# Rows laid out by position modulo four in a macaron block of routed experts and dilated attention

## The reference

```python
x = x + 0.5 * ffn(layernorm(x))      # "job" m = 0..7 in the kernel
x = x + long_attention(layernorm(x)) # "long"
x = x + 0.5 * ffn(layernorm(x))      # "job" m = 8..15

def ffn(x):                          # per sequence
    q, k, v = split(x @ w_qkv)       # 16 heads of 8
    o = softmax(causal(q k^T / sqrt(8))) v
    h = layernorm(x + o @ w_o) * g1 + b1
    w = top 2 of 8 experts of softmax(h @ wg), rescaled to sum 1
    moe = sum over the two: w * (gelu(h @ w1 + bb1) @ w2 + bb2)
    return layernorm(h + moe) * g2 + b2

def long_attention(x):               # q = k = v = x, one head of 128
    # the 256 positions split by position modulo 4 into 4 sets of 64;
    # each set: softmax(xs xs^T / sqrt(128)) xs, divided by 4
```

## Time and profile before

| | |
|---|---|
| median of 3 runs | 1218.78 us (1218.28 to 1222.53) |
| profiled execution | 1228.96 us, its span 1227.1 us |
| mean granted TensorE clock | 0.893 |
| TensorE matmuls | 1042.0 us busy, 85% of the span |
| TensorE weight loads | 837.6 us, 68% |
| VectorE | 693.5 us, 57% |
| ScalarE | 655.5 us, 53% |
| GpSimd | 586.3 us, 48% |
| DMA | 181.01 MB, mean 148 GB/s |

### The profile page before, as it was taken

The page is one execution under the profiler, slowest core; times in us unless marked ns, Lnnn a source line. Parts: engine busy times, 40 slices in busy tenths (PEclk is TensorE's granted clock), DMA queues, the critical chain, the costliest instruction groups (busy, mean ns, idle before and its releaser), DMA issues.

```text
span 1227.1 us, 29800 instructions
## 1 busy us (share of the span) xinstructions
PE 1042.0 (85%) x10977; PEld 837.6 (68%) x10977; DVE 693.5 (57%) x2452; ACT 655.5 (53%) x1478; POOL 586.3 (48%) x711
## 2 busy tenths in 40 slices
PE   4888979998989989898989979898899988776660
PEld 3566647886867777686767867787777866676660
DVE  6548656563568745685558835786557723520413
ACT  1233425774666656675656746666566747343240
POOL 2224455236555545546464555656364466443415
PEclk9878979997989988898988989999889979888685
DMA  4492116655545646544555545545456546576561
GB/s 80 97 210 60 37 35 171 196 164 147 155 151 133 187 117 171 137 124 162 147 145 156 159 127 148 161 147 172 127 158 174 169 138 180 165 247 221 169 213 45
DMA packets 116471, 181.01 MB, mean 148 GB/s; under 512 B 12360, under 2 KB 79464, under 8 KB 116328
## 3 DMA queue, kind: packets, MB, share of 16 engines
q1 hardware_dynamic: 108136, 162.32, 46.9%
q0 software_dynamic: 8192, 16.79, 4.8%
HBM read 145.10 MB, written 38.68 MB: 150 GB/s over the span
## 4 chain that ended last, share of the span: by engine, by line
PE 72%; DVE 8%; another core or an unknown queue 6%; issue 6%; ACT 5%; POOL 2%; DMA 1%; POOLq 0%; ACTq 0%; DVEq 0%
PE ps_ring L569 15%; PE ps_ring L578 12%; PE ps_quad L440 8%; PE ps_quad L473 6%; PE ps_quad L469 6%; PE ps_ring L486 5%; PE ps_quad L446 3%; PE ps_ring L490 2%; ACT probs L653 2%; PE ps_ring L413 2%; PE ps_ring L501 2%; PE ps_ring L560 2%; PE ps_ring L420 1%; POOL picked L1107 1%
## 5 line engine op out<-in xcount | busy, mean ns | idle before, releaser
L1045 POOL TENSOR_SCALAR_AFFINE_SELECT probs<-probs 128x512 f32<-128x512 f32 x256 | 178.7, 707 | 272.2 <-ACT probs L653 265.9
L653 ACT ACTIVATE probs<-ps_quad 128x768 f32<-128x768 f32 x256 | 194.0, 806 | 162.5 <-PE ps_quad L473 100.6
L689 ACT ACTIVATE act<-ps_ring,weights 128x128 f32<-128x128 f32 x736 | 201.8, 385 | 123.9 <-PE ps_ring L569 90.1
L816 DVE TENSOR_REDUCE shift_cols<-ps_quad 128x2 f32<-128x512 f32 (+3 forms) x256 | 149.9, 586 | 153.5 <-PE ps_quad L454 117.8
L578 PE MATMUL ps_ring<-weights,act 128*128 128x128 f32 x1472 | 202.3, 286 | 35.1 <-ACT act L689 18.8
L569 PE MATMUL ps_ring<-tile_t,weights 128*128 128x128 f32 x1472 | 199.6, 293 | 17.0 <-ACT tile_t L680 8.8
L578 PEld LDWEIGHTS ps_ring<-weights,act 128*128 128x128 f32 x1472 | 185.1, 199 | 38.5 <-ACT act L689 20.6
L569 PEld LDWEIGHTS ps_ring<-tile_t,weights 128*128 128x128 f32 x1472 | 185.7, 205 | 31.1 <-issue 18.3
L1107 POOL DMA_INDIRECT picked<-sorted_outputs,place x128 | 123.2, 962 | 81.9 <-issue 81.6
L941 DVE TENSOR_TENSOR tile_y<-ps_ring,weights 128x128 f32<-128x128 f32 x184 | 51.1, 287 | 191.8 <-PE ps_ring L578 97.5
L1094 POOL DMA_INDIRECT sorted_rows<-h_rows,place x128 | 124.0, 969 | 52.3 <-issue 34.5
(11 more groups left out here) (132 smaller groups left out, 1532.2 us busy)
## 6 DMA issues: line engine op xcount, KB each, us to landing
weights<-expert_weights SPq DMA_DIRECT2D x184, 578.0 KB
tile_rows<-sorted_rows SPq DMA_DIRECT2D x56, 192.0 KB
sorted_outputs<-tile_y SPq DMA_DIRECT2D x56, 192.0 KB
query_key_parts<-qk SPq DMA_DIRECT2D x32, 256.0 KB, 4.8
k<-query_key_parts SPq DMA_DIRECT2D x64, 64.0 KB
q<-query_key_parts SPq DMA_DIRECT2D x64, 64.0 KB
sorted_rows<-zeros SPq DMA_DIRECT2D x2, 1472.0 KB, 10.7
xs<-in_L_attn_x SPq DMA_DIRECT2D x8, 256.0 KB, 5.6
```

The lines of the kernel that those rows point to most:

```text
L653: sc.activation(probs[:, r % PROBS, 2 * a:2 * a + 2, :], ps_quad[:, 2 * a:2 * a + 2, 0:3 * P], ACT.Exp, scale=HD ** -0.5).then_inc(pair_fr ...
L689: ins = sc.activation(act[:, k % ACTS, f, :], bank(use)[:, f * P:(f + 1) * P], ACT.Gelu_apprx_tanh, bias=weights[:, k % WEIGHTS, 2 * F + f ...
L816: dve.tensor_reduce(shift_cols[:, late, groups], ps_quad[:, groups, 0:split], AX.X, ALU.max)
L1045: pool.affine_select(out=both, in_=both, compare_op=ALU.is_ge, fill=0.0, base=0, pattern=[[0, 2], [0, 2], [1, P]], channel_multiplier=-1). ...
```

## The change

Partition 64g + n of row tile 2q + h now holds position 4n + 2h + g of sequence q: a row tile holds two of the four remainders, one on partitions 0 to 63, one on 64 to 127. What follows from it:

- loads and stores of a chunk are four transfers of 64 KB (two halves of the partitions by two sequences) instead of one of 256 KB;
- ScalarE's copy to `xn_t` writes its columns in the order of positions (a step of four numbers between neighbours), and its copy to `attn_feat` goes back to the order of the row tiles (neighbours go 64 numbers apart);
- `long_scores` computes for each row tile its own 128 x 128 scores; the exp takes only the two diagonal 64 x 64 blocks, in two instructions on 64 partitions each; the other blocks of `long_e` are set to zero once at the start;
- `long_values` needs one product a row tile instead of two;
- the mask product on GpSimd and `phase_of` go.

Apart from this, jobs 14 and 15 end differently. For both, GpSimd's product with g2 is part of a VectorE instruction that also subtracts the mean, and the add to the residual multiplies by the reciprocal deviation. Job 15 is combined row tile by row tile, each with a semaphore of its own for its two gathers, and is stored in two halves.

```diff
-    x_tiles = x.rearrange("(c q) (h p) d -> c p (q h) d", q=2, p=P)
+    x_phases = x.rearrange("(c q) (n h g) d -> c g n q h d", q=2, h=2, g=2)
...
+            def load_chunk(c):
+                for g in range(2):
+                    for q in range(2):
+                        sp.dma_start(xs[PHASE * g:PHASE * g + PHASE, TT * c + 2 * q:TT * c + 2 * q + 2, :],
+                                     x_phases[c, g][:, q, :, :]).then_inc(x_in[c], 16)
...
+            def store_sequence(c, q):
+                for g in range(2):
+                    sp.dma_start(out_phases[c, g][:, q, :, :],
+                                 chunk_rows(c)[PHASE * g:PHASE * g + PHASE, 2 * q:2 * q + 2, :]).then_inc(stored, 16)
...
                 for kt in range(2):
-                    mm = pe.matmul(bank(use)[:, kt * S:(kt + 1) * S],
-                                   long_xn_t[:, b * S + kt * P:b * S + (kt + 1) * P],
-                                   long_xn_t[:, b * S:(b + 1) * S], start=True, stop=True)
+                    both = long_xn_t[:, b * S + kt * P:b * S + (kt + 1) * P]
+                    mm = pe.matmul(bank(use)[:, kt * P:(kt + 1) * P], both, both, start=True, stop=True)
...
-                pe.wait_ge(long_masked, 2 * c + b + 1)
+                freed(pe, ("long_scores", c, b))
                 take(pe, use)
                 for qt in range(2):
-                    for kt in range(2):
-                        mm = pe.matmul(bank(use)[:, qt * S:qt * S + D + 1],
-                                       long_e[:, b, kt, qt * P:(qt + 1) * P], long_xn[:, 2 * b + kt, 0:D + 1],
-                                       start=(kt == 0), stop=(kt == 1))
+                    mm = pe.matmul(bank(use)[:, qt * S:qt * S + D + 1], long_e[:, b, qt, :],
+                                   long_xn[:, 2 * b + qt, 0:D + 1], start=True, stop=True)
...
-                sc.activation(xn_t[:, :], bank(("turn", m)), ACT.Copy).then_inc(free_sem(("turn", m)), 1)
+                sc.activation(xn_t[:, :].rearrange("p (q n r) -> p q r n", q=2, r=RATE),
+                              bank(("turn", m)).rearrange("p (q r n) -> p q r n", q=2, r=RATE), ACT.Copy
+                              ).then_inc(free_sem(("turn", m)), 1)
...
-                sc.activation(attn_feat[:, :], bank(("merge", m)), ACT.Copy).then_inc(free_sem(("merge", m)), 1)
+                sc.activation(attn_feat[:, :].rearrange("p (q r n) -> p q n r", q=2, r=RATE),
+                              bank(("merge", m)).rearrange("p (q n r) -> p q n r", q=2, r=RATE), ACT.Copy
+                              ).then_inc(free_sem(("merge", m)), 1)
...
-                sc.activation(long_e[:, b, :, :].rearrange("p k q -> p (k q)"), bank(use), ACT.Exp, scale=D ** -0.5
-                              ).then_inc(free_sem(use), 1)
+                pairs = bank(use)[:, 0:S].rearrange("p (k q) -> p k q", k=2)
+                for r in range(2):
+                    at = slice(PHASE * r, PHASE * r + PHASE)
+                    ins = sc.activation(long_e[at, b, :, at], pairs[at, :, at], ACT.Exp, scale=D ** -0.5)
+                ins.then_inc(free_sem(use), 1)
...
+            def combine_last():
+                m = JOBS - 1
+                first, second = picked[:, m % 2, 0, :, :], picked[:, m % 2, 1, :, :]
+                for tt in range(TT):
+                    dve.wait_ge(last_rows_in[tt], 32)
+                    step(dve.scalar_tensor_tensor(out=first[:, tt, :], in0=first[:, tt, :],
+                                                  scalar=gates[:, m % 8, 0, tt:tt + 1], in1=h_rows[:, m % KEPT, tt, :],
+                                                  op0=ALU.mult, op1=ALU.add))
...
+                    step(dve.bn_stats(stats[:, END, tt, :], first[:, tt, :]))
+                    settle()
+                    step(dve.bn_aggr(moments[:, END, tt, :], stats[:, END, tt, :]))
+                    settle()
+                    if tt < TT - 1:
+                        dve.scalar_tensor_tensor(out=first[:, tt, :], in0=first[:, tt, :],
+                                                 scalar=moments[:, END, tt, 0:1], in1=g2_half[:, :],
+                                                 op0=ALU.subtract, op1=ALU.mult)
...
-            def long_scores(c, b):
-                freed(pool, ("long_scores", c, b))
-                pairs = long_e[:, b, :, :].rearrange("p k (n r) -> p (k n) r", r=RATE)
-                pool.tensor_tensor(pairs, pairs,
-                                   phase_of[:, :].unsqueeze(1).broadcast_to([P, 2 * S // RATE, RATE]), ALU.mult
-                                   ).then_inc(long_masked, 1)
```

More of the change, by code:

```diff
@@ new lines, in finish_last @@
+            def finish_last():
+                m = JOBS - 1
+                rows = picked[:, m % 2, 0, :, :]
+                dve.wait_ge(residual_ready, m + 1)
+                settle()
+                dve.wait_ge(rstd_ready[END], m + 1)
+                for tt in range(TT):
+                    out_rows = chunk_rows(m)[:, tt, :]
+                    ins = dve.scalar_tensor_tensor(out=out_rows, in0=rows[:, tt, :], scalar=rstd[:, END, tt:tt + 1],
+                                                   in1=out_rows, op0=ALU.mult, op1=ALU.add)
+                    if tt % 2:
+                        ins.then_inc(last_result, 1)
```

76 lines of the change are left out of this document (62 added, 14 removed).

## The result

The changed kernel takes 1203.88 us (median of 4 runs, 1202.10 to 1207.25); the kernel before, run beside it, 1219.52 us (4 runs, 1218.28 to 1222.53). The ratio is 0.9871, 95% interval 0.9843 to 0.9900: 15.6 us faster. I had forecast 1210 us, range 1201 to 1220, with faster at 0.62. The sum was -9.3 us; the runs show about six more.

The account below looks back on a forecast made before the run. TensorE was taken to bound the kernel, with 72% of the chain of waits. Terms -11.4 - 2.0 + 1.5 + 2.0 + 0.6 = -9.3 us led from 1218.78 to 1209.5 us, range 1201 to 1220.

Parts of the forecast that it names:

- TensorE's part: Long attention's score and value matmuls: 14.2 us less on the chain of waits, 80% taken: -11.4 us, bounds 0 and 18.0.
- 80% on the path: Share of the matmuls' 14.2 us on the chain counted as gain, as TensorE is busy nine tenths there: 11.4 us.
- GpSimd's part: Removed long-attention mask product, 16 times 1.036 us: hides behind TensorE, so counted zero; gain bounded by 16.6 us, loss excluded.
- ScalarE's part: Long attention's exps: no difference; 32 copies with stepped writes, 0.40 us more each: +2.0 us, bounds 0 and 83.
- two readings of the 16-byte step: Stepped xn_t copy: free by the Trainium skill's cacheline note (ScalarE term 0.6 us), or 0.40 us dearer (term 2.0).
- slower rival: Stepped copies at 3.2 us each, 83 us more on ScalarE, a third on the chain: 1235.5 us; chance 0.10.
- far row: Profile row of a reciprocal of 16 elements read 128 bytes apart, 253 ns: 6.25 ns an element, 3.2 us a copy.
- SyncE's part: Smaller transfers: +1.5 us at the first chunk's load, 0 for the six chunks behind, +0.6 for the last stage's stores.
- The tail: End of jobs 14 and 15: last power at 1217.2 instead of 1218.00, earlier last stores: -2.0 us, bounds 0.5 and 3.
- The base: Profiled 1228.96 us would become 1219.7; the 10.2 us difference between profiled run and median leads from 1218.78 to 1209.5.
- no change: In the dilated-attention stage shorter matmuls only wait longer, a fifth of 14.2 us remains: 1218.1 us; chance 0.25.
- The larger rival: Shift breaks all four 5.6 us waits behind the scatter bursts, 22 us go as well: 1188 us; chance 0.05.

Follow-up runs that it names:

- pe_restored: Changed kernel with TensorE's long score and value matmuls put back to the earlier columns and counts; 1194.80 us, ratio 0.9861 to the kernel before.
- both_restored: Changed kernel with both GpSimd's 16 mask products (and TensorE's waits on them) and TensorE's earlier long matmul work put back; 1209.28 us, ratio 1.0012 to the kernel before.
- pool_restored: Changed kernel with GpSimd's 16 mask products put back and TensorE's value matmuls waiting for them; 1204.06 us, ratio 0.9981 to the kernel before.
- pool_nowait: Changed kernel with GpSimd's 16 mask products put back but no TensorE wait on them; 1061.13 us, ratio 0.9920 to the kernel before (1070 us there).
- read_step: Changed kernel with ScalarE's two copies stepping through PSUM reads and writing SBUF in one run; 1190.46 us, ratio 0.9895 to the kernel before.
- tail_only: Kernel before with only the new end of the last two jobs, old layout kept; 1208.52 us, ratio 1.0003 to the kernel before.
- before_again: Kernel before, unchanged, run and profiled once more; median 1211.98 us, profiled execution 1214.57 us, ratio 1.0011.
- pe_restored_2: Changed kernel with TensorE's earlier long matmul work put back, run again on another chip; 1063.02 us, ratio 0.9909 to the kernel before (1071 us there).
- layout_only: Changed kernel with the old end of the last two jobs, new row layout kept; 1192.63 us, ratio 0.9870 to the kernel before.

## Why the prediction was right, and where it was not

The time and the verdict were right; that the sum came so near is partly luck, since two of its terms were wrong in opposite directions. The steps, in their order:

- **TensorE's part, -11.4 us.** The durations of the records were right: 17.9 us less busy time (18.0 to 11.3, and 23.9 to 12.7) against 7.2 + 10.8 worked out for all groups. What failed is the 80% on the path. On the first kind of chip pe_restored measures 0 to 8 us where I had 11.4 (and both_restored against pool_restored 3.7, give or take 6); on the chips of 1070 us, where TensorE is busy over 99% of a set, the term counts, as a part of the 8.6 us that pool_nowait gains; but even there the matmuls put back add only 0.8 to 2.1 us of busy time a set, 3 to 8 in all. The chain of waits ran through TensorE 72% of the time, but a chain names who was last, not who would be last if that one were faster.
- **GpSimd's part, 0.** This is the step that failed most. pool_restored measures 13 us of the bound of 16.6 that I had given and set aside, with the words that the product is cover for nothing and hides behind TensorE. I had even written what stands behind it, the place list and the scatters, and not priced that both would come earlier. No product was on the chain; its time was on the path all the same. It is not TensorE's wait for the product, which had ended 7.3 us or more before each matmul that waits for it; it is in part VectorE, whose place list was 1.17 us a set late beside the products. pool_nowait, which drops the wait, ran on the other kind of chip only.
- **ScalarE's part, exps 0 and copies +2.0.** The exps went from 9.6 to 8.6 us, a miss of 1 us within the bounds. A copy costs 0.48 us more, and I took 0.40. Of the prediction's two readings of the 16-byte step, nothing and 0.40 us, the runs bear out the second. read_step finds no gain from taking it back, with an interval of about 10 us, which allows the +2.0 as well as 0. The slower rival (3.2 us a copy) is dead. Two of the rows were read too freely: 365 against 264 ns is 1.4 times the run and not twice, and the reciprocal of the far row reads PSUM where its neighbour reads SBUF, so that it could say nothing of steps in SBUF.
- **SyncE's part, +1.5, 0 and +0.6.** The first statistics came 1.39 us later, as forecast (5.12; forecast 5.2), and the first projection 1.87 later with the longer copy. The 24 loads ended ahead of the next issue: 0 was right. The rule of the Trainium skill, "DMA: Bandwidth & Descriptors", rules for kernel authors, would have had the 48 extra transfers serialize; the 24 went out at 0.67 us an issue (16.13 / 24) beside other work, and the trace shows no cost of theirs but the first. No run separates the stores' +0.6.
- **The tail, -2.0.** 0.83 of the 0.8 us up to the power came; behind it 0.4 instead of 1.2, since job 15's four small issues take 0.62 us each, 2.48 in all, where I had 2.0, and the adds start 1.20 us after the power where I had 1.06. 1.2 in all, below what tail_only can tell.
- **The base.** Leading the profiled 1228.96 us to the median by one difference was right: by before_again the profiled execution was most likely a long one.

The rivals: *no change* rested on the shorter matmuls bringing only a fifth of 14.2 us, 2.8. That fits what they brought on the first kind of chip (0 to 8), and the forecast was saved by GpSimd's term. The larger rival, all four 5.6 us waits gone, did not come; TensorE still stops behind the scatters.

## What to carry to other kernels

A chain that runs 72% through one engine does not price work taken from another. For every engine that stands ahead of a burst or a list that is waited for, keep its removed time as a term with a chance, not as a bound only; here it was 13 of the 15.6 us. Look too at what the other engines do while it works: here short VectorE instructions took three to six times as long beside a GpSimd product. Look whether the engine you shorten has idle time in the same stretch: at 92 busy of 100 us its own gain was mostly absorbed, at 99.5 it counted, though for less than the sum of its records. And put back each part alone: the sum was near, the parts were not.

## What the runs showed of the hardware that I had not expected

- Chips differ by 12%: the kernel before takes 1209 us on two and 1070 us on two others. The same kernel on one of each (pe_restored and pe_restored_2) has the same busy times on ScalarE (669.4 and 669.0 us), VectorE (680.5 and 682.1) and nearly on GpSimd (572.0 and 575.9); TensorE's differ (1019.8 and 939.9), with the clock (0.917 and 0.950). Why TensorE stops in the bursts on the first kind is open.
- TensorE's mean granted clock is not fixed for a kernel. With its work put back it rose from 0.899 to 0.913 (means of six runs each, layout_only and pe_restored), and the busy time grew by 8.6 us for 24.5 us of matmul records (47.4 against 22.9). This is no rule: with GpSimd's products in place the same work left it at 0.903 (0.904 without it; twelve runs each, both_restored and pool_restored).
- A ScalarE copy of 128x512 fp32 takes 0.60 us in one run, 1.09 writing SBUF in steps of 16 bytes, 1.08 in steps of 256, and 0.61 with the step on the PSUM side.
- A VectorE instruction of 1x23 elements takes 0.17 us, and 0.97 when a GpSimd product of 128x512 (1.04 us) starts just before it; one of 128x4 takes 0.17, and up to 1.01 (L755 in before_again, beside a product). Reduces of 128x512 beside a product keep their 0.68 us.
